# One core, a sandwich of self-attention and a ternary feed-forward network over 16 batches: four kinds of instruction are re-ordered in the first batches, and one rounding of a weight part goes from ScalarE to GpSimd

## What is computed

```python
def _L0_attn_ref(x, w_lhs, w_rhs):
    lhs, rhs = x * w_lhs, x * w_rhs
    scores = jnp.einsum('nsd,ntd->nst', lhs, rhs)
    return jnp.einsum('nst,ntd->nsd', jax.nn.softmax(scores, axis=2), x)

def _L0_ffn_ref(x, ...):                      # 128 -> 512 -> 512 -> 512 -> 128
    h = silu(_tlin(x, w1_w, w1_s)) * _tlin(x, w2_w, w2_s)
    h = gelu(_tlin(h, h1_w, h1_s)); h = gelu(_tlin(h, h2_w, h2_s))
    return _tlin(h, w3_w, w3_s)

x = x + _layernorm(_L0_attn_ref(_layernorm(x), w_lhs, w_rhs))
x = x + _layernorm(_L0_ffn_ref(_layernorm(x), ...))
```

## Time and profile before

| | us | share of the span |
|---|---|---|
| median of three runs | 496.38 | |
| the profiled execution's own time | 496.54 | |
| its span in the trace | 494.8 | |
| TensorE busy | 477.8 | 97% |
| ScalarE busy | 450.2 | 91% |
| VectorE busy | 395.8 | 80% |
| GpSimd busy | 235.1 | 48% |

### The profile page before, as it was taken

How to read it: one execution, slowest core, us unless ns; L and a number is a source line. 1 busy time by engine, 2 the same in 40 slices (tenths; PEclk the granted TensorE clock), 3 DMA queues, 4 the chain that set the end, 5 groups by cost and what they waited for, 6 DMA issues and landing times.

```text
span 494.8 us, 9479 instructions
## 1 busy us (share of the span) xinstructions
PE 477.8 (97%) x2850; PEld 388.7 (79%) x2850; DVE 395.8 (80%) x1179; ACT 450.2 (91%) x780; POOL 235.1 (48%) x257
## 2 busy tenths in 40 slices
PE   7789999999999999999999999999999999999994
PEld 6567788888888888888888888888888888888783
DVE  5999889796987969689696978969596878757565
ACT  4799999999999999999999999999999899996963
POOL 4475764635254563534556254463705434463531
PEclk9999999999999999999999999999999999999998
DMA  8022002110203011020301103020030020310012
GB/s 288 32 66 85 2 15 72 43 43 7 101 0 106 0 48 58 1 105 0 106 0 42 64 0 106 1 95 33 1 86 1 0 87 0 87 44 1 1 44 88
DMA packets 12845, 24.23 MB, mean 49 GB/s; under 512 B 1552, under 2 KB 2064, under 8 KB 12816
## 3 DMA queue, kind: packets, MB, share of 16 engines
q1 hardware_dynamic: 12816, 23.87, 14.8%
HBM read 15.48 MB, written 8.39 MB: 48 GB/s over the span
## 4 chain that ended last, share of the span: by engine, by line
PE 86%; DVE 6%; ACT 2%; issue 1%; POOL 0%; DVEq 0%; ACTq 0%; POOLq 0%
PE hid_bank L377 23%; PE hid_bank L379 23%; PE score_bank L313 5%; PE hid_bank L398 3%; PE hid_bank L402 3%; PE hid_bank L403 3%; PE hid_bank L399 3%; PE w_bank L377 3%; PE w_bank L379 3%; PE mix_bank L363 3%; PE w_bank L322 2%; PE mix_bank L367 2%; PE mix_bank L364 2%; PE score_bank L345 2%; PE score_bank L351 2%; PE score_bank L348 2%
## 5 line engine op out<-in xcount | busy, mean ns | idle before, releaser
L377 PE MATMUL hid_bank<-hA_hi,w_hi 128*128 128x512 f32 x256 | 106.3, 415 | 0.1
L377 PE MATMUL hid_bank<-hB_hi,w_hi 128*128 128x512 f32 x256 | 103.8, 405 | 0.0
L379 PE MATMUL hid_bank<-hA_lo,w_hi 128*128 128x512 f32 x256 | 101.3, 396 | 0.0
L379 PE MATMUL hid_bank<-hB_lo,w_hi 128*128 128x512 f32 x256 | 101.1, 395 | 0.0
L2233 POOL TENSOR_TENSOR hC_lo<-hC_full,hC_hi 128x512 fp32r<-128x512 f32 x60 | 76.9, 1296 | 19.2 <-ACT hC_full L1230 19.0
L1180 ACT ACT_TABLE_LOAD x51 | 65.4, 1283 | 1.6 <-PEq L2409 0.7
L1591 DVE SCALAR_TENSOR_TENSOR hA_full<-hid_bank,columns,gate 128x512 f32<-128x512 f32 x64 | 47.4, 748 | 16.4 <-ACT gate L1223 15.8
L379 PEld LDWEIGHTS hid_bank<-hB_lo,w_hi 128*128 128x128 f32 x256 | 48.3, 189 | 10.1 <-DVE hB_lo L1742 0.4
L377 PEld LDWEIGHTS hid_bank<-hB_hi,w_hi 128*128 128x128 f32 x256 | 48.2, 188 | 9.9 <-DVE hB_lo L1742 0.2
L379 PEld LDWEIGHTS hid_bank<-hA_lo,w_hi 128*128 128x128 f32 x256 | 48.4, 189 | 8.9 <-DVE hA_lo L1738 0.3
L377 PEld LDWEIGHTS hid_bank<-hA_hi,w_hi 128*128 128x128 f32 x256 | 48.3, 188 | 9.1 <-DVE hA_full L1591 0.5
(11 more groups left out here) (147 smaller groups left out, 1203.6 us busy)
## 6 DMA issues: line engine op xcount, KB each, us to landing
x_res<-x_dram SPq DMA_DIRECT2D x16, 256.0 KB, 2.7
out_dram<-x SPq DMA_DIRECT2D x16, 256.0 KB, 2.0
x_tail<-out_dram SPq DMA_DIRECT2D x16, 256.0 KB, 2.7
out_dram<-y_out SPq DMA_DIRECT2D x15, 256.0 KB, 3.0
x_in<-x_dram SPq DMA_DIRECT2D x14, 256.0 KB, 2.8
w_raw<-weights_dram SPq DMA_DIRECT2D x5, 512.0 KB, 6.7
x_in<-x_dram SPq DMA_DIRECT2D x2, 128.0 KB, 2.2
x_ahead<-x_dram SPq DMA_DIRECT2D x1, 256.0 KB, 3.1
```

Source lines behind the costliest of these rows:

```text
L377: nc.tensor.matmul(bank[:, :], w_hi[:, w], hi, start=first, stop=False)
L379: mm = nc.tensor.matmul(bank[:, :], w_hi[:, w], lo, start=False, stop=last and not general)
```

## The change

Seven edits, all to the order of the lists. On TensorE, `attend(0, 0)` now stands behind all four `turn_e(0, j)`. On ScalarE, `sum_lo(0)` goes ahead of `softmax(0, 0)`; `softmax(0, 2)` goes ahead of `high_e(0, 0)`; `sum_lo(2)` goes from behind `high_e(1, 2)` to behind `sum_lo(3)`; `high_weights(1)` leaves ScalarE. On VectorE, `x_statistics(2)` goes behind the four `row_max(0, j)`; `low_aT(1)` and `low_aT(2)` follow `low_xT(1)` and `low_xT(2)` directly; `row_max(1, 0)` and `row_max(1, 1)` are set around `aggregate(ln_att, 0)`. On GpSimd, `high_weights(1)` comes in behind `high_weights(2)`. The loop and the end stay as they are.

```diff
                 turn_e(0, 0)
                 turn_e(0, 1)
-                attend(0, 0)
                 turn_e(0, 2)
                 turn_e(0, 3)
+                attend(0, 0)
                 pe.wait_ge(xT_lo_ready, 2)
...
                 high_weights(0)
+                sum_lo(0)
                 softmax(0, 0)
-                sum_lo(0)
                 softmax(0, 1)
+                softmax(0, 2)
                 high_e(0, 0)
-                softmax(0, 2)
                 softmax(0, 3)
...
                 sum_lo(1)
                 sum_lo(3)
+                sum_lo(2)
                 softmax(1, 0)
...
                 high_e(1, 2)
-                sum_lo(2)
                 sum_lo(5)
                 sum_lo(4)
-                high_weights(1)
                 high_e(1, 3)
...
                 row_max(0, 1)
-                x_statistics(2)
                 row_max(0, 2)
                 row_max(0, 3)
+                x_statistics(2)
                 low_e(0, 0)
...
                 low_xT(1)
+                low_aT(1)
                 high_xn(1)
                 attention_statistics(0)
-                low_aT(1)
+                row_max(1, 0)
                 aggregate(ln_att, 0)
+                row_max(1, 1)
                 normalize_x(2, 0)
-                row_max(1, 0)
-                row_max(1, 1)
                 normalize_x(2, 1)
...
                 low_xT(2)
+                low_aT(2)
                 x1_statistics(0)
-                low_aT(2)
                 aggregate(ln_x1, 0)
...
                 rstd(ln_x, 1)
                 high_weights(2)
+                high_weights(1)
                 high_weights(5)
                 high_weights(4)
```

## The result

The changed kernel takes 500.92 us (median of 4 runs, 500.68 to 501.33) against 496.39 for the kernel before on the same chip: ratio 1.0089, 95% interval 1.0072 to 1.0107. It is slower by 4.5 us. The forecast was 499.9 us, with 497.3 to 501.0 as its range; the narrower range that it gave for its likeliest case, 499.2 to 500.8, misses the median by 0.1 us. In all that follows medians are of all executions and ratios of the fast ones alone, so that a ratio is not exactly the quotient of its medians (in experiment 9 it is 1.0002 beside 496.01 against 496.37), and one slow execution of 531.53 us in the second timing of experiment 8 is in its median and not in its ratio.

A forecast was written before the change was run, and what follows sets the result against it. TensorE, nearly gapless from 34 us, passes any shift of `turn_x2(0)` to the end. Gains of 0.2 and 0.3 us against a 4.1 us loss added 3.6 to 496.54, less 0 to 0.4 for gaps: 499.9 us, range 497.3 to 501.0.

The forecast's parts named there:

- likeliest case: At `x2n` of batch 0, VectorE and GpSimd take turns after each instruction: 3.6 us net loss, 499.2 to 500.8 us, 66%.
- What bounds the kernel: TensorE has next to no gap from 34 us on; a shift of `turn_x2(0)` goes to the end nearly one for one.
- TensorE's gap ahead of `gated(0, 2)`: TensorE's small gaps after 34 us were to give back 0 to 0.4 us of the delay.
- Stage 1: VectorE up to batch 1's normalization: arrives at 14.16 instead of 15.28, meets two GpSimd casts, gains 0.2 us.
- the sum: Adds VectorE's gains of 0.2 and 0.3 us against 4.1 us lost at `x2n`: 3.6 us net loss.
- Stage 2: VectorE up to the statistics of `x1`: re-ordered maxima and low parts gain 0.3 us; moving `sum_lo(2)` costs nothing.
- Stage 3: At `x2n` of batch 0: `low_weights(1)` starts ahead of VectorE, it and `low_weights(4)` hold tiles; loss 4.1 us, 3.6 net.
- VectorE keeps the port: Two rivals, VectorE holding on through a run: in Stage 3 only, 497.8 us, 10%; also in Stage 1, 496.2 us, 10%.
- The faster case: Rival: at `x2n`, `low_weights(1)` starts after VectorE's tiles began or doesn't collide: 495.9 to 495.0 us, or 494.3; 9%.

The follow-up runs named there:

- experiment 9: Kernel before with `high_weights(1)` moved to GpSimd and `low_weights(1)` waiting for `x2n` of batch 0, none of the re-orderings: 496.01 us, ratio 1.0002.
- experiment 8: Changed kernel with `low_weights(1)` waiting for `x2n`, and GpSimd's casts of parts 5 and 4 moved behind `rstd_att(0)`: 495.13 us, in a second timing 495.34 us.
- experiment 1: Kernel before with one edit alone, `high_weights(1)` moved from ScalarE to GpSimd behind `high_weights(2)`: 501.3 us, ratio 1.0102.
- experiment 6: Changed kernel with one more wait on GpSimd, `low_weights(1)` waiting until `x2n` of batch 0 is written: 495.66 us, ratio 0.9992.
- experiment 2: Changed kernel with `high_weights(1)` back on ScalarE behind `sum_lo(4)`, all other edits kept: 501.21 us, ratio 1.0098.
- experiment 3: Changed kernel with `high_weights(1)` and `sum_lo(2)` both back at their old places on ScalarE, the other edits kept: 498.78 us, ratio 1.0052.
- experiment 4: Changed kernel without `low_weights(4)`, so one low part is not computed: 497.99 us, ratio 1.0041.
- experiment 7: Changed kernel with matmuls that nobody reads on TensorE while it waits for `x2n` of batch 0: 500.01 us, ratio 1.0084.
- experiment 10: Kernel before with `high_weights(1)` on GpSimd, `low_weights(1)` waiting for `x2n`, casts of parts 5 and 4 behind `rstd_att(0)`, no re-orderings: 496.86 us, ratio 1.0007.

## Why the prediction was right, point by point

- **What bounds the kernel.** Right. The delay at `turn_x2(0)` and the clock behind it went on to the end, 4.6 us at 204 us and 4.2 at the end of the profiled execution. TensorE's gap ahead of `gated(0, 2)` gave nothing back; it grew, from 0.24 to 0.58 us. From the first `gated` matmul to the end of the trace it is 459.9 us in the kernel before and 459.7 in the changed one, and 459.2 to 460.5 in the traces of all the experiments: what a version costs is decided when `gated(0, 0)` begins.
- **Stage 1.** The arrival at 14.16 (measured 14.19) and the collision with the casts were right. The last tile of `xn` starts 0.69 us earlier (16.12 against 16.81) and not 0.2. Of this, 0.18 us are the casts' earlier end, 16.05 against 16.23. The other 0.51 were a slip of the sum: in the kernel before three tiles started behind the casts' end, now only one does, and the forecast's own picture, two tiles done before the casts and turns after, already has these two times 0.26 us in it.
- **Stage 2.** VectorE reaches the statistics' aggregation 0.85 us earlier against a sum of 0.5. As experiment 1 shows 0.75 us with VectorE's list untouched, the two traces can't judge this term, and experiments 6 and 9 give 0.1 to 0.5 us of time for it, with overlapping intervals. One price in this stage was right only by the company it kept: moving `sum_lo(2)` was put at nothing, but with the cast still on ScalarE it lets the cast, and so GpSimd, come early, and the whole loss is there (experiment 2).
- **Stage 3.** The mechanism and its order were as forecast: `low_weights(1)` ahead of VectorE (by 0.30, forecast 0.26), tile 0 after the first, tiles 1 to 3 after the second. `x2n` ended 7.08 us after the start of the aggregation, forecast 7.35: two `low_weights` together took 4.64 us, where the sum had 4.88 (2.40 each and 0.08 between them). The 4.80 of before seem to hold a short wait for VectorE's last tile, which was running at 32.49; no run separates it. Net, `x2n` is 3.0 us late against 3.6 forecast.
- **What the sum left out.** It named no clock, and the section on the time before says that no time depends on it; that held for the kernel before and not for the changed one. Everything after 40 us was to be 3.5 us later and is 4.6 later. The missing term is 1.4 us of work at half clock behind the wait, shown by the traces of experiments 3, 4 and 7. The smaller `x2n` delay and the missing clock partly cancel. That 499.9 came as near as 1.0 us is in part luck: with the forecast's own 3.6 us and the clock's 1.4, it would have been 501.3, above its range.
- **The rivals.** That VectorE keeps the port is refuted by the changed kernel itself, where two tiles of four are held, and by experiment 3, where one tile of a run is caught. The faster case needed GpSimd to start behind VectorE. Forced by a wait it removes the loss; that it ends below the kernel before, by 0.4 us in experiment 6, is not clear of the noise. A rival was missing: that the other re-orderings, with the cast left where it was, would let GpSimd catch tiles as well (experiments 2 and 3).

The Trainium skill, "SBUF — State Buffer", section "Who interferes with whom", says that where the two contend for the port pair that they share, whoever issues first has it for the whole instruction and the other blocks fully. The tiles' 2.90 and 4.94 us and the single tile caught in experiment 3 agree with it. That what they share is a port, no run here shows; the runs show that a tile caught by a `low_weights` ends 0.08 to 0.09 us behind it.

## What to carry to other kernels

A wait can be doing work: before taking one away from an engine, look at which instruction behind it is let go, and what that one shares with the critical path. A long elementwise instruction on GpSimd costs VectorE little by its mere presence: in experiment 6, two `low_weights` run from 32.49 to 37.21 beside VectorE's maxima and subtractions, which take their usual 0.68 us. But it costs up to its whole length when a short VectorE instruction of the blocked kind arrives just after it, and each further one can do so again (1.8 and 2.0 us here for two of 2.3 us). A wait on the critical result ahead of it is the cheap cure. And where TensorE is made to wait, count also the work behind the wait at half clock: 1.4 us here, behind a wait of 1.96 us (experiment 3) and one of 4.3 us (the changed kernel).

## What the runs showed of the hardware that was not expected

- TensorE's granted clock fell in the changed kernel while TensorE stood between 30.4 and 35.2 us, and its transposes and small matmuls then ran at half pace: eight `attend` matmuls start 0.11 us apart, where it was 0.06 in the kernel before. When it fell differs from trace to trace: in experiment 1, where `x2n` is as late, it was still 1.00 until 36 us and 0.51 on average from 36 to 39. These are TensorE's windows there:

```profile
33.00:36.00 3.00, 0.96 (x4) 1.00 0.00 0
36.00:39.00 3.00, 3.00 (x28) 0.51 0.01 3
```

  The price was nearly the same all the same, since the work behind the wait fell into that stretch: `gated` followed `x2n` by 3.42 us there and by 3.58 in the changed kernel. In experiment 4 the clock fell sooner, and was back when `x2n` was ready. TensorE's windows there:

```profile
28.00:31.00 3.00, 3.00 (x11) 0.50 0.64 223
31.00:34.00 3.00, 1.61 (x18) 0.95 0.00 0
34.00:37.00 3.00, 2.99 (x33) 1.00 0.01 3
```

  So the price hangs on which work falls into the low stretch. In the fastest version (experiment 8, second trace) the clock was 0.53 from 26 to 29 us, ahead of `x2n`, and cost nothing that can be seen.
- Work that nobody reads, put into the wait, kept the clock up and shortened what came behind it, from 3.58 to 2.14 us (experiment 7).
- Not every GpSimd instruction holds such a tile. In the kernel before, the power of an `rstd` takes 1.01 us, and a tile of `xn` that starts 0.09 us into it takes 0.34 us as if alone:

```profile
92.07 1.01 POOL L2224 TENSOR_TENSOR ln_att_rstd<-ln_att_var_eps,minus_half 128x4 f32<-128x4 f32 x1
92.16 0.34 DVE L1753 TENSOR_SCALAR xn<-x_in,ln_x_mean_var,ln_x_rstd 128x128 f32<-128x128 f32 x1
```

- The first loads don't end at the same time in each trace. VectorE's statistics of batch 2's `x` started at 12.70 in the kernel before, at 11.95 in experiment 9 and at 11.98 in experiment 10, with VectorE waiting for the load in each. GpSimd, waiting for the last weight parts in both, started their casts at 14.63 in the kernel before and at 13.88 in experiment 9.
